# A graph kernel's first edge loop in fixed blocks of 14 tiles and five passes, with a reordered preparation

## What is computed

```python
def _L0_gnn_ref(X, edge_index, ...):
    q = (X @ Wq).reshape(N, H, DH)
    k = (X @ Wk).reshape(N, H, DH)
    v = (X @ Wv).reshape(N, H, DH)
    scores = jnp.einsum('ehd,ehd->eh', q[dst], k[src]) / jnp.sqrt(jnp.float32(DH))
    m = jax.ops.segment_max(scores, dst, num_segments=N)
    ex = jnp.exp(scores - m[dst])
    denom = jax.ops.segment_sum(ex, dst, num_segments=N)
    alpha = ex / (denom[dst] + 1e-09)
    agg = jax.ops.segment_sum(alpha[:, :, None] * v[src], dst, num_segments=N)
    embedding = agg.reshape(N, D) @ W0
    h1 = _layer_norm(X + embedding, ln1_g, ln1_b)
    ff = jax.nn.relu(h1 @ fc1_w + fc1_b) @ fc2_w + fc2_b
    return _layer_norm(h1 + ff, ln2_g, ln2_b)
...
    x = _layernorm(x + _L0_gnn_ref(x, edge_index, ...), axis=-1)
    x = _layernorm(x + _L1_gnn_ref(x, edge_index, edge_attr_16, ...), axis=-1)
```

## Time and profile before

| | us |
|---|---|
| median of 3 runs | 2734.34 |
| lowest, highest | 2734.33, 2736.21 |
| profiled execution | 2738.81 |
| its span | 2737.0 |

### The profile page before, as it was taken

One profiled execution on the slowest core, in us unless ns is written; L12 is line 12 of the kernel. 1 busy time (PEld: TensorE's weight loads), 2 busy tenths in 40 slices (PEclk: granted clock), 3 DMA queues, 4 the chain that ended last, 5 costly groups with the idle time before them and its releaser, 6 DMA issues.

```text
span 2737.0 us, 36397 instructions
## 1 busy us (share of the span) xinstructions
PE 1670.2 (61%) x9440; PEld 1270.3 (46%) x9441; DVE 1500.4 (55%) x3221; ACT 538.4 (20%) x1401; POOL 1817.3 (66%) x1690
## 2 busy tenths in 40 slices
PE   0535666666666666666647875666666666666665
PEld 0424555555555555555545653444444434444443
DVE  2644666666666666666658972344444444444443
ACT  0431111111111111111112331111111111111111
POOL 1027777777777777777751115777777777777775
PEclk9866777777777777777768996777777777777777
DMA  3414333333333333333310112222222222222221
GB/s 102 154 55 96 96 94 94 94 95 95 95 94 96 95 94 95 96 95 94 96 40 13 37 38 53 57 60 58 60 60 59 59 60 58 59 60 58 59 59 47
DMA packets 161868, 203.94 MB, mean 75 GB/s; under 512 B 77391, under 2 KB 121819, under 8 KB 161711
## 3 DMA queue, kind: packets, MB, share of 16 engines
q0 software_dynamic: 65888, 162.90, 21.6%
q1 hardware_dynamic: 92046, 39.37, 5.7%
q10 hardware_dynamic: 3908, 1.38, 0.2%
HBM read 184.85 MB, written 25.06 MB: 77 GB/s over the span
## 4 chain that ended last, share of the span: by engine, by line
POOL 52%; issue 22%; DMA 12%; DVE 6%; PE 4%; SPq 3%; ACT 1%; DVEq 0%; POOLq 0%; ACTq 0%
POOL arena L581 30%; POOL arena L629 22%; DMA arena<-y_tab,arena 5%; DMA kv_tab<-arena 3%; DMA arena<-i 2%; SPq L349 1%; DVE arena L1513 1%; PE ps L1073 1%; SPq L471 1%; DVE arena L1423 1%; PE ps L1033 1%; DVE arena L1413 1%; DMA keeps<-arena 0%; DMA i<-arena 0%; PE ps L1007 0%
## 5 line engine op out<-in xcount | busy, mean ns | idle before, releaser
L581 POOL DMA_INDIRECT arena<-kv_tab,arena x850 | 936.8, 1102 | 287.5 <-issue 258.6
L629 POOL DMA_INDIRECT arena<-y_tab,arena x784 | 813.1, 1037 | 262.2 <-issue 238.6
L971 PE MATMUL ps<-arena 128*128 x2550 | 268.1, 275 | 287.8 <-ACT arena L740 211.3
L1121 PEld LDWEIGHTS ps<-arena 128*128 128x128 f32 x1568 | 275.2, 256 | 326.7 <-ACT arena L849 275.4
L1121 PE MATMUL ps<-arena 128*128 128x128 f32 x1568 | 306.7, 353 | 158.8 <-ACT arena L849 158.7
L1513 DVE TENSOR_TENSOR arena<-ps,arena 128x512 f32<-128x512 f32 x224 | 139.5, 623 | 453.1 <-DMA arena<-y_tab,arena 453.1
L971 PEld LDWEIGHTS ps<-arena 128*128 128x128 bf16 x2550 | 224.9, 126 | 339.1 <-ACT arena L740 290.5
L849 ACT ACTIVATE arena<-arena 128x512 f32<-128x512 f32 x224 | 129.0, 576 | 864.4 <-DVE arena L1513 864.4
L1007 PEld LDWEIGHTS ps<-arena 128*128 128x128 f32 x1600 | 275.3, 260 | 0.0
L961 PE MATMUL ps<-ident,arena 128*128 128x128 f32 x850 | 159.4, 319 | 189.7 <-DVE arena L1327 189.7
L1007 PE MATMUL ps<-arena 128*128 128x136 f32 x1600 | 273.6, 348 | 0.0
(11 more groups left out here) (242 smaller groups left out, 2163.2 us busy)
## 6 DMA issues: line engine op xcount, KB each, us to landing
arena<-kv_tab,arena POOLq DMA_INDIRECT x850, 2.8
arena<-y_tab,arena POOLq DMA_INDIRECT x784, 2.5
eat<-ea SPq DMA_DIRECT2D x59, 112.0 KB, 2.0
ea<-in_edge_attr_dram SPq DMA_DIRECT2D x2, 3125.0 KB, 22.3
kv_tab<-arena SPq DMA_DIRECT2D x10, 625.0 KB
y_tab<-arena SPq DMA_DIRECT2D x20, 312.5 KB
out_dram<-arena SPq DMA_DIRECT2D x56, 64.0 KB, 1.9
xs<-in_x_dram SPq DMA_DIRECT2D x1, 3125.0 KB
```

The lines of the kernel that those rows point to most:

```text
L581: g.indirect_dma_start(kv_s[:, u, t, :], None, kv_tab, bass.IndirectOffsetOnAxis(ap=v3(idx, 2)[:, u, t:t + 1], axis=0)).then_inc(l_g[u][k] ...
L629: g.indirect_dma_start(yg_s[:, r, t, :], None, y_tab, bass.IndirectOffsetOnAxis(ap=v3(idx1, 2)[:, u, t:t + 1], axis=0)).then_inc(m_g[r][k] ...
L971: last = mm(bank(x_)[:, t * D:(t + 1) * D], st_s[:, x_, t * P:(t + 1) * P], qsp[:, ds(tile + part * D, D)], start=(part == 0), stop=(part ...
L1121: last = mm(bank(6 + u)[:, 0:W], yg_s[:, r, t, :], hot1_s[:, u, t, :], start=(t == 0), stop=(t == G1 - 1))
```

## The change

Layer 0's edge loop works like that of layer 1: 56 blocks of 14 tiles (1792 edges), cut without regard to nodes, each with a window of 128 nodes from its first edge's node on (`nodes`, features on the partitions). The gathered rows have a ring of four chunks. Five passes are in work: `new` (scores in four pieces, maxima within lanes), `a_` (maxima across lanes), `b_` (differences, masks, weighted values, sums on PE), `c_` (`averages`: the part of a node that spans two blocks is carried over, and the division by the sum of exponentials), `e_` (ACT stores the window). Masks (L1388 of after) and weighted values (L1396) are four instructions each, of 512, 384, 512 and 384 columns. The transposed masks are made by ACT (`lane_masks`, two instructions of 1792 columns) from a line of the block's dst that SP sends to all 128 partitions (`load_line`, 918 KB a chunk, one buffer `dstb`); the transposes on PE go. Queries are float32 products with a window of 128 rows that is loaded from a new table `q_tab` (64 KB a chunk). `steps` and `lanes` (DVE) form the marks of a node's first edge from dst, where `pen0` was loaded before.

In the preparation dst and src are loaded first on ACT's queue, x in five pieces whose rows are 5 KB, node 50p + t being row p of tile t, so that stores have rows of 5 KB too. One product of 384 columns makes query, key and value; ACT and DVE copy alternate tiles; three store buffers. Counts and the shifted copy of dst go; the table needs the dst of each block's first edge (56 numbers). The table of layer 1 is made here too. The copy of the edge attributes comes onto SP's queue ahead of the passes of layer 0. In the middle the division and its transposes go, `normalise` of the first and third norm moves to ACT (`normalised`), and the buffer of y is doubled. The layer-1 loop keeps its instructions.

```diff
-G0 = 17
-CH0 = G0 * P
-QUADS = ((0, 4), (4, 4), (8, 3), (11, 3), (14, 3))
...
+G = 14
+CH = G * P
...
+PIECES = ((0, 4), (4, 3), (7, 4), (11, 3))
+NP_ = len(PIECES)
+PVA = 7
+HW = H * G
+RING = 4
...
-            sp.wait_ge(s_zero, 1)
-            sp.dma_start(v3(xs[:, :], TILES)[0:NT], x.rearrange("(t p) d -> p t d", p=NT)).then_inc(s_x, 16)
-            sp.dma_start(v3(dsti, 2)[0:EP], dst_halves).then_inc(s_dst, 16)
-            sp.dma_start(v3(srci, 2)[0:EP], src_halves).then_inc(s_dst, 16)
...
+            x_rows = x.rearrange("(p t) d -> p t d", t=TILES)
+            span = 2 * GRP
+            for k in range(GROUPS // 2):
+                sp.dma_start(v3(xs[:, :], TILES)[0:NT, k * span:(k + 1) * span, :], x_rows[:, k * span:(k + 1) * span, :]).then_inc(s_x[k], 16)
...
+            sp.wait_ge(s_pre, 1)
+            sp.dma_start(d0[1:1 + E].rearrange("(h p c) -> p h c", h=2, c=EQ), v3(dstf, 2)[0:EP]).then_inc(s_d0, 16)
+            sp.wait_ge(s_d0, 48)
+            marks = lambda a: a[0:NB * CH].rearrange("(b c) -> b c", c=CH)[:, 0:1]
+            sp.dma_start(firsts[0].rearrange("(b c) -> b c", c=1), marks(d0[1:1 + NB * CH]), allow_slow_non_contiguous=True).then_inc(s_first[0], 16)
...
-                             ea[h * HALF:(h + 1) * HALF, :].rearrange("(p c) f -> p (c f)", p=EP)).then_inc(s_eac, 16)
...
-            with sp.Fori(0, GROUPS) as i:
-                sp.wait_ge(s_kvst, i + 2)
-                sp.dma_start(kv_tab[ds(i * (GRP * NT), GRP * NT), :].rearrange("(t p) d -> p t d", p=NT),
-                             v3(kvst[:, ds((i % 2) * (GRP * 2 * D), GRP * 2 * D)], GRP)[0:NT]).then_inc(s_kvo, 16)
-                sp.wait_ge(s_kvo, 16 * i + 16)
-                sp.sem_inc(s_kvfree, 1)
...
+            def store_rows(i):
+                u = i % KVR
+                sp.wait_ge(s_ca, acts(i * GRP + GRP - 1))
+                sp.wait_ge(s_cv, vecs(i * GRP + GRP - 1))
+                sp.dma_start(by_row(kv_tab, i * GRP, GRP), kvst_s[0:NT, u, :, D:QKV]).then_inc(s_kvo[u], 16)
+                sp.dma_start(by_row(q_tab, i * GRP, GRP), kvst_s[0:NT, u, :, 0:D]).then_inc(s_kvo[u], 16)
+            for i in range(GROUPS):
+                store_rows(i)
+                if i == 2:
+                    store_table(0)
+                    sp.wait_ge(s_ea, 16 * 10)
+                    sp.dma_start(firsts[1].rearrange("(b c) -> b c", c=1), marks(d1), allow_slow_non_contiguous=True).then_inc(s_first[1], 16)
+                if i == 3:
+                    load_table(0)
+                    sp.wait_ge(s_first[1], 16)
+                    spread(1)
+                if i == 7:
+                    store_table(1)
+                if i == 8:
+                    load_table(1)
...
+            def load_line(chunk):
+                off = entry0(chunk, 0, NB * CH)
+                sp.dma_start(dstb, d0[ds(off, DB)].rearrange("(a n) -> a n", a=1).to_broadcast([P, DB])).then_inc(l_db, 16)
...
+            def sp_edges(r, new, a_, b_, c_, e_):
+                if new is None:
+                    return
+                u = r % 2
+                if b_ is not None:
+                    sp.wait_ge(s_d0, 48)
+                    sp.wait_ge(l_dcr, picked)
+                load_heads(new + 2, (r + 2) % RING)
+                sp.wait_ge(s_arr, 16 * 3)
+                sp.wait_ge(l_ml, ended)
+                load_index(new + 4, r)
+                sp.wait_ge(s_d0, 48)
+                sp.wait_ge(l_hT, formed)
+                load_line(new + 3)
+                sp.wait_ge(s_arr, 16 * 3)
+                sp.wait_ge(l_q, asked)
+                load_queries(new + 3, 1 - u)
...
+            load_queries(2, 0)
+            for h in range(2):
+                sp.dma_start(ea1[h * BASE1:h * BASE1 + HALF, :].rearrange("(p c) f -> p (c f)", p=EP),
+                             ea[h * HALF:(h + 1) * HALF, :].rearrange("(p c) f -> p (c f)", p=EP)).then_inc(s_eac, 16)
+            passes4(sp, sp_edges, n0, 4)
...
+            act.dma_start(v3(dsti, 2)[0:EP], dst_halves).then_inc(s_dst, 16)
+            act.dma_start(v3(srci, 2)[0:EP], src_halves).then_inc(s_dst, 16)
...
+            def lane_masks(chunk, u, r):
+                act.wait_ge(l_paq, plus2)
+                pq_ = v3(paq, RING)[0:H, r, :]
+                a.activation(pq_, pq_, ACT.Copy, scale=-BIG).then_inc(l_paqc, 1)
+                line = dstb[:, 1:CH + 1]
+                a.activation(line, line, ACT.Square, bias=njc[:, ds(chunk, 1)]).then_inc(l_sq, 1)
+                act.wait_ge(l_sq, plus2)
+                if asked_from(chunk):
+                    act.wait_ge(l_q, asked)
+                a.activation(ucol[:, ds(chunk, 1)], line[:, CH - 1:CH], ACT.Relu, scale=-1.0, bias=1.0)
+                a.activation(hotT.rearrange("n (u g e) -> n u g e", u=2, g=G)[:, u, :, :], line.rearrange("n (e g) -> n g e", g=G),
+                             ACT.Relu, scale=-1.0, bias=1.0).then_inc(l_hT, 1)
...
-                if old is not None:
-                    dve.wait_ge(l_e, last_)
-                    ts(contrib[0:1, 0:H], contrib[0:1, 0:H], -1.0, None, ALU.add)
-                    for s0, s1, done in ((0, PVA, l_pva), (PVA, G0, l_pvb)):
-                        tt(rows_[:, s0:s1, :, 0:DH], kv_s[:, w, s0:s1, D:2 * D].rearrange("p g (h w) -> p g h w", h=H),
-                           rows_[:, s0:s1, :, DH:AW].to_broadcast([P, s1 - s0, H, DH]), ALU.mult).then_inc(done, 1)
...
-                if new is not None:
-                    scores(u, 3)
-                if old is not None:
-                    dve.wait_ge(l_rsc, last_)
-                    at = atmp.rearrange("p (h w) -> p h w", h=H)
-                    link(tt(at, cur_s[:, u, :].rearrange("p (h w) -> p h w", h=H), rsc[:, :, None].to_broadcast([P, H, AW]), ALU.mult))
...
-                if new is not None:
-                    dve_prep(w, now)
-                    scores(u, 4)
...
+            def averages(u, r, c_):
+                sums = cur_s[:, u, :].rearrange("p (h w) -> p h w", h=H)
+                dve.wait_ge(l_cur, minus3)
+                if not (type(c_) is int and c_ == 0):
+                    dve.wait_ge(l_ra, minus4)
+                    dve.wait_ge(l_avT, minus4)
+                    link(stt(ctmp[0:1, :].rearrange("p (h w) -> p h w", h=H), bank(7)[0:1, W:W + RW].rearrange("p (h w) -> p h w", h=H),
+                             hot_s[0:1, u, 0, 0:1], fac_s[0:1, r, :, None].to_broadcast([1, H, AW]), ALU.mult, ALU.mult))
+                    link(tt(cur_s[0:1, u, :], cur_s[0:1, u, :], ctmp[0:1, :], ALU.add))
+                link(ts(rden, sums[:, :, DH], 1e-9, None, ALU.add))
+                link(v.reciprocal(rden, rden))
+                tt(av.rearrange("p (h w) -> p h w", h=H), sums[:, :, 0:DH], rden[:, :, None].to_broadcast([P, H, DH]), ALU.mult).then_inc(l_av, 1)
...
+            def masks(u):
+                dve.wait_ge(l_dcr, minus2)
+                for s0, n in PIECES:
+                    last = tt(hot_s[:, u, s0:s0 + n, :], iota_row[:, None, :].to_broadcast([P, n, P]),
+                              dcr_s[:, u, s0:s0 + n, None].to_broadcast([P, n, P]), ALU.is_equal)
+                last.then_inc(l_hot, 1)
+            def weighted(u, r):
+                dve.wait_ge(l_e, minus2)
+                for s0, n in PIECES:
+                    s1 = s0 + n
+                    last = tt(contrib_s[:, u, s0:s1, :, 0:DH], kv_s[:, r, s0:s1, D:2 * D].rearrange("p g (h w) -> p g h w", h=H),
+                              contrib_s[:, u, s0:s1, :, DH:AW].to_broadcast([P, n, H, DH]), ALU.mult)
+                    if s1 in (PVA, G):
+                        last.then_inc(l_pva if s1 == PVA else l_pvb, 1)
+            def dve_edges(r, new, a_, b_, c_, e_):
+                u = r % 2
+                if new is not None:
+                    scores(r, 0)
+                if b_ is not None:
+                    differences((r + 2) % RING)
+                if new is not None:
+                    scores(r, 1)
+                if a_ is not None:
+                    across((r + 3) % RING)
+                if c_ is not None:
+                    averages(1 - u, (r + 1) % RING, c_)
+                if new is not None:
+                    steps(1 - u, (r + 1) % RING)
+                    lanes((r + 2) % RING)
+                if b_ is not None:
+                    masks(u)
+                    weighted(u, (r + 2) % RING)
+                if new is not None:
+                    scores(r, 2)
+                    scores(r, 3)
+                    local_max(r)
...
-                    sums = acc0[:, ds(new * (GRP * RW), GRP * RW)].rearrange("p (t h w) -> p t h w", t=GRP, h=H)
-                    link(ts(rd, sums[:, :, :, DH], 1e-9, None, ALU.add))
-                    link(v.reciprocal(rd, rd))
-                    tt(a4, sums[:, :, :, 0:DH], rd[:, :, :, None].to_broadcast([P, GRP, H, DH]), ALU.mult).then_inc(n_a, 1)
```

1122 lines of the change are left out of this document (533 added, 589 removed).

## The result

The changed kernel takes 2744.84 us (median of 7 runs, 2741.45 to 2748.77), the kernel before 2734.34 (7 runs beside them): the ratio is 1.0035, with a 95% interval from 1.0024 to 1.0046. It is slower by 0.35%, where 2625 us had been forecast, and it lies outside the range of 2505 to 2705.

A forecast was written before the change was run, and what follows sets the result against it. POOL's gathers, held up by touching DVE instructions with two SBUF inputs, were taken to bound both loops. From 2738.8 us, -96 + 20 + 6 - 39 = -109 gives 2629.8, set to 2625 against the median; range 2505 to 2705.

The forecast's parts named there:

- Loop of layer 0: Layer 0's edge loop: one gather a chunk held through all eight touching DVE pieces, period 21.7 us, +20 us.
- The rule of the pages: Skill's shared-pair rule would admit a gather after the piece holding it; forecast instead a hold through all touching pieces.
- Preparation: Before the first gather: first store at 20 us, ten groups of 7.5, first gather at 105; -96 us.
- Drain: Last gather of layer 0 to the middle: two more passes run out, +6 us (0 to +10).
- Middle: Between the loops: memset wait, layer 1's table and division go, normalisation on ACT costs 0; -39 us (-25 to -50).
- Rivals 1 and 2: Layer 0's loop: 1, POOL slips in between pieces, 2452 us, 0.08; 2, run breaks at a wait, 2508 us, 0.15.
- Rival 3: Layer 0's loop: line load sets the period, up to 26.7 us, whole 2905; chance 0.11, of which 0.06 slower.
- Rival 4: Preparation and middle save half: stores at 10.3 us, middle -25, table waited for; 57 us more, 2682; chance 0.06.

The follow-up runs named there:

- e1_coarse: Changed kernel with masks in one instruction of 1792 columns and weighted values in two of 896, instead of four each: 2719.8 us.
- e2_waits: Changed kernel with a wait on the piece before ahead of each of the eight pieces of masks and weighted values: 2569.9 us.
- e3_apart: Changed kernel with the scores of piece 2, whose product reads PSUM, between masks and weighted values: 2653.2 us.
- e9_stores_first: Changed kernel with later weight loads, longer store pieces, reordered SP loads, and groups 0 and 1 stored ahead of the dst wait: 3276.6 us, on a slower chip.
- e4_norm_dve: Changed kernel with the first and third normalisation of the middle made by DVE again: 2723.2 us.

## Why the prediction was wrong, point by point

**Loop of layer 0: right.** The period was given as 21.7 us with one stall of 4.2; it is 21.40 with one of 4.1 in 54 of 56 chunks, and ends 0.82 to 0.83 us behind the run. The run is 5.3 us as the rows above have it, 4.9 were summed: `lanes` is 0.58 and not 0.39, and the averages' product and the eight pieces are 0.08 and 0.09 longer. Over the 54 long gathers the start lies 1.0 us into the run in the mean, within the 0.65 to 1.07 assumed. The means given for the kernel before stand the wrong way round (1.39 us too much beside the masks, 1.29 beside the pair), which changes neither that range nor the sum. That splitting does not free POOL is shown by e1_coarse, that touching is the cause by e2_waits and e3_apart. The stage came out 17.5 us shorter than forecast.

**The rule of the pages.** The Trainium skill, SBUF — State Buffer, section Who interferes with whom, calls the shared pair an exclusive lock and says of DVE's 2-port modes that whoever issues first gets it for the whole instruction; the prediction read that for two SBUF inputs too. Here a gather was held over eight instructions, and over three, as long as they touched, and for one once they did not. The trace agrees with the sentence only where there is a gap.

**Preparation: the step that failed most.** I took a first store at 20 us, ten groups of 7.5 us, and 5 to 10 us behind the last: 105. Measured: the first store at 57 us, 98 us from there to the last, and 17 us behind it: 172.5. All three terms were too small, by 37, 23 and some 10 us. What the first had left out are two chains of some 50 us, ACT's issues of weight loads and SP's store and reload of dst; with both out of the way the first store went out at 25.1 us. The second rested on rows of 5 KB and on a table whose load lies "under the stores". The queries between the nodes' keys and values broke the rows into pieces of 1 KB, and longer pieces gave 15 us back. And the table stands in DVE's code ahead of the third group's copies: in e9_stores_first the wait for it took up the whole head start. Of the edits, earlier issues, another order behind the last store, and early stores gave nothing or 2 to 3 us; 3.1 MB less gave 22.

One comparison would have warned me: my 105 us needed 107 x 172.5/105 = 176 GB/s for the bytes that the changed kernel moves, where the earlier trace rows had 105 in the mean. I costed waits one behind the other and took the queue of transfers behind them for free. The change takes 6.25 MB of the edge attributes' copy out of the stage and adds 3.1 MB of queries; 3.1 MB net at 105 GB/s would be about the 28.6 us that were gained. That the stage lasts as long as its bytes is not shown, though: whether it is the bytes or the waits for landings stays open, and other bytes, such as x's, were not tried.

**Drain.** +14 for the +6 forecast: two more passes with nothing between them, 6.4 us of sums on PE in the last. The mechanism was as said, the size wrong: the term of 6 us measured 14.

**Middle: two steps failed.** The normalisation on ACT "at what they took on DVE: 0" was wrong: its ten instructions (3.96 us) stand ahead of the copy on which PE waits, and e4_norm_dve gave 19 us back. And the 2.5 us of division that DVE lost did not come off the interval: with the norms back and the copy moved back it stands at 18.5, as before with 18.3, though DVE is busy 14.6 us of it for 16.9, and the chain runs through PE and ACT alone. In the kernel before the chain of a group runs through DVE's row for 10 us (1543.6 to 1553.4). So a chain through PE and ACT of nearly the same length took over; that it lay there before the change is inferred, not measured. I had named PE as next "at some 15 of 16 us" from its busy time, which says nothing of the ACT copies between its products. PE's clock adds to it where it falls: the ten products of L1109 took 2.43 us at 1452.91 at a granted clock of 1.00 and 4.11 us at 1474.38 at 0.58 (the levels of 2.4 and mostly 1.2 GHz), after 1.7 us in which PE waited for ACT in both cases; what made the one fall and not the other stays open.

**The rivals.** Rivals 1 and 2 were refuted for this code, both by the one long gather. Rival 3, the line load, did not set the loop on the chip of the changed kernel: it landed in 5.4 us in the median, where 8.6 to 12.1 had been reckoned. Only in the first 100 us of the loop did DVE stand for it at L1329, 7 times and 30.7 us in all, with a longest landing of 22.0 us. Rival 4 had the right place and only half the size: it gave 57 us to preparation and middle, they took 67 + 57 more.

## What to carry to other kernels

Where one engine waits for another engine's run of instructions, the length of a run without a gap counts, not the length or the number of its instructions: a gap of 0.03 us between pieces was worth 171 us of the loop here, and 88 us of it in the kernel before. On the chips where both loops take longer it was worth nothing, or cost time, so it is to be measured on the chip that will run the kernel. Before costing the waits of a stage full of transfers, divide its bytes by the forecast time and compare the rate with that which the trace shows; and look in each engine's code for what stands between the pieces that are to overlap, as the table did here. And before work is moved to an idle engine, look for the copy that stands behind it on that engine and for who waits for that.
